# Two sets of product banks in the projections, and two transposing banks and two reciprocal buffers when heads are brought back to nodes

## The reference, cut to what matters

```
# first network (graph convolution)
h = h @ W                                        # here (W1 W2) in one, 256 -> 64, scaled by node
# second and fourth network (attention with H heads of 64; H = 4 and H = 2)
proj = (x @ gat_w.T).reshape(n, H, 64)
s_src = jnp.sum(proj * gat_a_src, -1); s_tgt = jnp.sum(proj * gat_a_tgt, -1)
e     = leaky_relu(s_src[src] + s_tgt[tgt], 0.2);  exp_e = jnp.exp(e - max)
denom = segment_sum(exp_e, tgt)
attn  = exp_e / denom[tgt]
agg   = segment_sum(proj[src] * attn, tgt)       # numerator and denominator are summed apart,
                                                 # and divided once per node
```

## Time and profile before

| | us |
|---|---|
| median of 3 runs (7667.7 to 7686.64) | 7669.45 |
| the profiled execution's own time | 7670.31 |
| its span, first to last instruction | 7668.7 |

### The profile page before, as it was taken

The page is one execution under the profiler, slowest core; times in us unless marked ns, Lnnn a source line. Parts: engine busy times, 40 slices in busy tenths (PEclk is TensorE's granted clock), DMA queues, the critical chain, the costliest instruction groups (busy, mean ns, idle before and its releaser), DMA issues. The chain is left out here.

```text
span 7668.7 us, 88070 instructions
## 1 busy us (share of the span) xinstructions
PE 4482.8 (58%) x19066; PEld 2333.8 (30%) x19067; DVE 4067.2 (53%) x6157; ACT 1802.2 (24%) x2723; POOL 2135.1 (28%) x2216
## 2 busy tenths in 40 slices
PE   4887575309992454549656776556775444430583
PEld 2553574104431122435222333223332121220121
DVE  8976473989984986335222333223331111128895
ACT  1565011108863221334101111001110000010352
POOL 0000000400000000100466665666665666630000
PEclk9998687659995677879777888678886566665797
DMA  1471674326652554235555656555665444453443
GB/s 40 162 235 54 218 252 145 136 85 191 180 159 88 223 220 164 86 103 210 166 163 173 195 186 192 156 161 183 191 203 145 139 136 139 137 134 117 137 134 108
DMA packets 496020, 1197.33 MB, mean 156 GB/s; under 512 B 65578, under 2 KB 288629, under 8 KB 475090
## 3 DMA queue, kind: packets, MB, share of 16 engines
q1 hardware_dynamic: 321342, 586.57, 23.7%
q0 software_dynamic: 141200, 464.73, 20.5%
q10 hardware_dynamic: 33396, 145.09, 5.2%
HBM read 924.69 MB, written 274.66 MB: 156 GB/s over the span
## 5 line engine op out<-in xcount | busy, mean ns | idle before, releaser
L2586 POOL DMA_INDIRECT rel1s_rows<-rel_table,rel1s_at x672 | 651.4, 969 | 396.4 <-issue 349.9
L2586 POOL DMA_INDIRECT rel0s_rows<-rel_table,rel0s_at x672 | 652.1, 970 | 376.1 <-issue 341.1
L2586 POOL DMA_INDIRECT rel2s_rows<-rel_table,rel2s_at x672 | 643.5, 958 | 371.6 <-issue 327.9
L2718 PE MATMUL rel2s_acc<-rel2s_rows,rel2s_hot 128*128 x764 | 407.1, 546 | 471.0 <-issue 409.6
L1677 PE MATMUL gatx_acc<-gatx_w,gatx_feat 128*65 128x400 f32 x1600 | 541.6, 501 | 25.7 <-DVE gatx_w L1569 25.7
L2718 PE MATMUL rel0s_acc<-rel0s_rows,rel0s_hot 128*128 x764 | 349.4, 473 | 295.7 <-issue 231.0
L2718 PE MATMUL rel1s_acc<-rel1s_rows,rel1s_hot 128*128 x764 | 348.5, 472 | 291.9 <-issue 222.1
L2240 POOL DMA_INDIRECT mixa_y<-y_sorted,g_rank x25 | 23.7, 949 | 1532.0 <-issue 1532.0
L2150 PE MATMUL mamb_acc<-mamb_st,g_ident 128*128 128x512 f32 (+1 forms) x448 | 252.5, 729 | 213.9 <-DVE mamb_st L2141 213.9
L1569 DVE SCALAR_TENSOR_TENSOR gatx_w<-gatx_w,gatx_adj 128x1600 f32<-128x1600 f32 x200 | 363.2, 1817 | 0.5 <-ACT gatx_w L1625 0.5
L1416 DVE CUSTOM_DVE_ANT_0 gatm_junk<-gatm_srow,gatm_gone 128x3200 bf16<-128x3200 f32 x100 | 343.5, 3488 | 33.5 <-DMA gatm_srow<-gat_scores 29.1
(11 more groups left out here) (609 smaller groups left out, 9619.5 us busy)
## 6 DMA issues: line engine op xcount, KB each, us to landing
mamb_bc<-dbc SPq DMA_DIRECT2D x64, 1600.0 KB, 6.6
agg_strip<-strips SPq DMA_DIRECT2D x100, 800.0 KB, 5.9
gatx_adj<-adj SPq DMA_DIRECT2D x200, 400.0 KB, 3.1
adj<-adj_counts SPq DMA_DIRECT2D x25, 1600.0 KB, 7.1
latx_adj<-adj SPq DMA_DIRECT2D x100, 400.0 KB, 3.1
rel_table<-rel0p_prod POOLq DMA_DIRECT2D x25, 1536.0 KB, 6.3
rel_table<-rel0s_prod ACTq DMA_DIRECT2D x25, 1536.0 KB
rel_table<-rel1s_prod ACTq DMA_DIRECT2D x25, 1536.0 KB
```

Source lines behind the costliest of these rows:

```text
L2586: pool.indirect_dma_start(rows[:, u, k, :], None, table, bass.IndirectOffsetOnAxis(ap=at[:, n:n + 1], axis=0)).then_inc(s_in[u], 16)
L2718: one = nc.tensor.matmul(acc[a][:, :], to, row[:, 0:2 * D], start=fresh and k == 0, stop=False)
```

## The change

Projections get two sets of product banks, used in turn by the tile's parity. `s_done` starts at `2 * NC`, so that a product waits for DVE's move of tile t-2 in place of t-1; POOL's wait is raised by the same `NC`, so that it still waits for its own tile. In `heads_to_nodes` PE's semaphore `s_o` starts at 1, so that PE waits for tile t-2 in place of t-1, and the reciprocals have a buffer per parity. No instruction is added, removed or put in another order on any engine but the one that sets `s_o`; the lines after 1722 move by up to two.

```
         tp = [ph.ps(f"tp{u}", [P, D]) for u in range(2)]
-        mm = [ph.ps(f"mm{n}", [P, BANK]) for n in range(NC)]
+        mm = [[ph.ps(f"mm{u}_{n}", [P, BANK]) for n in range(NC)] for u in range(2)]
...
             pe.sem_inc(s_tp, 2)
-            pe.sem_inc(s_done, NC)
+            pe.sem_inc(s_done, 2 * NC)
...
                     pe.wait_ge(s_done, t * NC + (n + 1))
                     for k in range(2):
-                        last = nc.tensor.matmul(mm[n][:, 0:b - a], turned[u][:, k, :], weights[:, k, a:b],
+                        last = nc.tensor.matmul(mm[u][n][:, 0:b - a], turned[u][:, k, :], weights[:, k, a:b],
                                                 start=k == 0, stop=k == 1)
...
-                        last = nc.vector.tensor_scalar(res[u][:, a:b], mm[n][:, 0:b - a], scale[:, bass.ds(t, 1)], None, ALU.mult)
+                        last = nc.vector.tensor_scalar(res[u][:, a:b], mm[u][n][:, 0:b - a], scale[:, bass.ds(t, 1)], None, ALU.mult)
...
             def step(t, i, u):
-                pool.wait_ge(s_done, (t + 2) * NC)
+                pool.wait_ge(s_done, (t + 3) * NC)
                 for to, out in store(t, res[u]):
...
         part = [ph.sb(f"part{u}", [65, H, P]) for u in range(2)]
-        den = ph.sb("den", [P, H])
+        dens = [ph.sb(f"den{u}", [P, H]) for u in range(2)]
         tp = [ph.ps(f"tp{u}", [P, BANK]) for u in range(2)]
...
             pe.sem_inc(s_t, 2)
+            pe.sem_inc(s_o, 1)
 
             def step(t, i, u):
                 pe.wait_ge(s_in[u], (i + 1) * 16)
                 pe.wait_ge(s_o, t)
...
             def step(t, i, u):
                 dve.wait_ge(s_t, t + 3)
+                den = dens[u]
```

More of the change, by code:

```diff
@@ L815, in step @@
                         nc.vector.tensor_copy(res[u][:, 0:heads * 65].rearrange("p (h c) -> p h c", c=65)[:, :, 0:64],
-                                              mm[n][:, 0:heads * 64].rearrange("p (h c) -> p h c", c=64))
+                                              mm[u][n][:, 0:heads * 64].rearrange("p (h c) -> p h c", c=64))
                         nc.vector.tensor_copy(extra[:, bass.ds(t, 1), :].rearrange("p a c -> p (a c)"),
-                                              mm[n][:, heads * 64:width])
-                        last = nc.vector.tensor_copy(res[u][:, heads * 65:], mm[n][:, heads * 64:width])
+                                              mm[u][n][:, heads * 64:width])
+                        last = nc.vector.tensor_copy(res[u][:, heads * 65:], mm[u][n][:, heads * 64:width])
                     elif scale is not None:
-                        last = nc.vector.tensor_scalar(res[u][:, a:b], mm[n][:, 0:b - a], scale[:, bass.ds(t, 1)], None, ALU.mult)
+                        last = nc.vector.tensor_scalar(res[u][:, a:b], mm[u][n][:, 0:b - a], scale[:, bass.ds(t, 1)], None, ALU.mult)
                     else:
-                        last = nc.vector.tensor_copy(res[u][:, a:b], mm[n][:, 0:b - a])
+                        last = nc.vector.tensor_copy(res[u][:, a:b], mm[u][n][:, 0:b - a])
                     last.then_inc(s_done, 1)
```

## The result

The changed kernel takes 7658.34 us (median of 20 runs), the kernel before 7670.02 in the same comparison (20 runs). The ratio is 0.9983, 95% interval 0.9976 to 0.9990, so 8 to 18 us less. The profiled execution took 7656.09, its span is 7654.4, 14.3 us under the 7668.7 of before.

A forecast was written before the change was run, and what follows sets the result against it. Bank waits for tile t-1 bounded the stages (`lasp` already its stores), leaving two-buffer load and store loops. Gains 3.6 + 1.4 + 0.5 + 6.2 + 1.3 = 13.0 us gave a median of 7656.5, range 7645 to 7671.

The forecast's parts named there:

- the rival with the Trainium skill's durations: Heads: loads take 2.0 us fixed plus bytes; `lash` gains nothing, `loch` 4.9 us, sum 10.4, median 7659; chance 0.05.
- `locp`: Projection stage: period falls from 1.88 us to its store loop, 3.64 for two tiles or 1.82 each; gain 1.4 us.
- `loch`: Heads stage: period falls from 1.85 us to its load loop, 3.18 for two tiles or 1.59 each; gain 6.2 us.
- the store loop of `gcnp`: Move, POOL's store issue, landing, move two tiles later: 2.95 us for two tiles, 1.48 per tile.
- the load loop of `lash`: Transposes, SP's load issue, landing, transposes two tiles later: 2.62 us for two tiles, 1.31 per tile; gain 1.3 us.
- `gcnp` and `lasp`: Projection stages: `gcnp` from 1.65 to 1.50 us per tile, gain 3.6; `lasp` already at its store loop, 1.77, gain 0.5.
- The banks as the only limit: All five stages: loads and stores follow, DVE bounds the heads and PE the projections; some 67 us, 7602; chance 0.03.
- The full clock in the heads: TensorE leaves 0.50 clock in `loch` and `lash`, transposes about 0.35 us not 0.69; 19 us in all, 7650.5; chance 0.08.
- The lost clock in `locp`: PE stays at 1.2 GHz in `locp`, 2.38 us per tile; 12 us lost in place of 1.4 gained, 7670; chance 0.05.
- The collision: Projections: loads and stores collide on the same 16 DMA engines and land later; 8.0 us slower, 7677.5; chance 0.05.
- my signs of being wrong: `loch`'s transposes name DVE, its loads land under 1.9 us, projections' stores later than 2.6, or untouched stages move over a few us.
- an engine's own work: Floor per tile if banks alone had limited: PE 1.33 us in `gcnp`, DVE 1.0 in `loch` and 0.9 in `lash`.

The follow-up runs named there:

- the second run of the projections alone: Only the projections changed, heads as in the kernel before; second comparison, on another chip: ratio 0.9989 to the kernel before (first comparison 1.0002).
- one buffer of reciprocals: The changed kernel with one reciprocal buffer in the heads, DVE waiting for its own previous multiplication: ratio 0.9979 to the kernel before.
- four result buffers: The changed kernel with four result buffers in the projections, so four stores in flight, and two load buffers: ratio 0.9958 to the kernel before.
- all deep without the change: Four load buffers in all five stages and four result buffers in the projections, but one set of product banks and heads one tile at a time: ratio 0.9986.
- the deep kernel: The changed kernel with four load and four result buffers in the projections and four load buffers in the heads: 7579.52 us against 7669.91, ratio 0.9885.

## Why the prediction was right

**The forecast** was 7656.5 and the measured median 7658.34; the gain forecast 13.0, measured 14.3 in the profiles and 11.7 in the medians. The median alone doesn't bear the mechanism out: its interval, 8 to 18 us, holds the forecast's 13.0 as well as the 10.4 of the rival with the Trainium skill's durations. The waits, the stages and the experiments do. That the sum came so close is in part luck, since two terms missed in opposite directions: `locp` by +1.9 us and `loch` by -0.9.

**The loops.** For two tiles, the store loop of `gcnp` was put at 2.95, that of `locp` at 3.64, the load loop of `lash` at 2.62, and measured are 2.95, 3.65 and 2.61. The one of `gcnp`:

```profile
824.72 0.28 DVE L821 TENSOR_SCALAR gcnp_res<-gcnp_mm,g_dinv 128x64 f32<-128x64 f32 x1 [1.45 <-DMA gcn_y<-gcnp_res]
...
827.67 0.28 DVE L821 TENSOR_SCALAR gcnp_res<-gcnp_mm,g_dinv 128x64 f32<-128x64 f32 x1 [1.41 <-DMA gcn_y<-gcnp_res]
```

For a landing that no view gave I had taken the data's end plus a wait seen elsewhere. In `lash` that held; in `loch` it was 0.13 us too short.

**`loch`** was put at 3.18 and is 3.30: 5.3 us gained in place of 6.2. From the transposes to the issue of the load it takes 0.92 as reckoned; what is longer is from the issue at 2300.61 to the transposes that use it at 2302.99, 2.38 in place of 2.25.

**`locp`** is the term that was mis-sized: 3.3 in place of 1.4 (2.0 to 3.4 over the kernels of the table). The period after was right (1.80 against 1.82); before, I read 1.88 in the middle of the stage where the mean is 1.94. Half of the gain lies in the first period alone. Before, then changed:

```profile
1262.44 0.42 DVE L815 COPY locp_res<-locp_mm 128x256 f32<-128x256 f32 x1 [5.22 <-PE locp_mm L784]
...
1265.29 0.42 DVE L815 COPY locp_res<-locp_mm 128x256 f32<-128x256 f32 x1 [2.28 <-PE locp_mm L784]
```

```profile
1257.92 0.42 DVE L815 COPY locp_res<-locp_mm 128x256 f32<-128x256 f32 x1 [5.22 <-PE locp_mm L784]
1258.02 1.06 PE L784 MATMUL locp_mm<-local_weights,locp_turned 128*128 128x264 f32 x4
...
1259.11 0.42 DVE L815 COPY locp_res<-locp_mm 128x256 f32<-128x256 f32 x1 [0.62 <-PE locp_mm L784]
```

That period falls from 2.85 to 1.19 us, by 1.66; the other 23 give 1.69 together, 0.07 each, where 0.06 was forecast. Of the 1.66, 1.04 is the clock: the second product took 2.10 us at 1.2 GHz before and 1.06 here, where the granted clock was 0.99 from 1257.9 on. It is not shown that the change brings this about. Of the nine kernels with two sets of banks, this product is at full speed in three (the changed one, the second run of the projections alone, one buffer of reciprocals) and takes 1.71 to 1.97 in the others; of the three with one set it takes 1.64 to 2.10. So up to 1 us of the gain may be luck, and the second bank's own part of the first period is some 0.6: 2.20 with a product of 1.97 (four result buffers) against 2.77 with one of 2.02 (all deep without the change). A stage's gain needs its own length, first to last, for the time before, and not the steady period alone.

**`gcnp` and `lasp`**: 3.6 and 0.6 us, put at 3.6 and 0.5. In `gcnp` both periods were read 0.03 us too short (1.65 and 1.50, means of 1.68 and 1.53), which cancels in the difference. `lasp` was said to be at its store loop already; before the change 14 of its 25 moves waited for the store and now 20 do. That its number fits is luck, with a stage that varies by 1.8 us between kernels that are the same there.

**The rivals.** The banks as the only limit: false, but only the deep kernels show by how much, since with four buffers the same banks are worth 77 us (ratios 0.9885 against 0.9986, of 7670), and with two of each 14. The full clock in the heads: `loch` stays at 0.50 even in the deep kernel, with transposes of 0.69. The lost clock in `locp`: it has 0.92 of full in the changed kernel, 0.93 before. The collision: the longest landing of `locp`'s stores did rise, from 2.6 to 3.3, and by its letter that is one of my signs of being wrong, "if the projections' stores land later than 2.6". The sign was badly chosen: before the change `lasp`'s longest was 3.1 already, and what counts over 24 periods is the median, which fell from 2.3 to 2.2. The other signs did not appear: the transposes of `loch` name their load, and the stretches between the touched stages moved by 2.0 us at most. The durations of the Trainium skill: `lash` gained 1.6 us where by them there was nothing to gain. The 2.15 us that I took from "DMA: Bandwidth & Descriptors" of the Trainium skill, "Anatomy of one DMA", is too long for this load by at least 0.1 us. But that section gives its fit for DMAs that GpSimd issues, and SP issues these, so I had no ground for applying it and the miss doesn't speak against the section. For `loch` the same rule came nearer than my own term: 3.29 for two tiles, where I forecast 3.18 and 3.30 was measured.

**My estimate of an engine's own work was too high.** For PE in `gcnp` I had 1.33 and the deep kernel shows 1.16 at the same clock: the overlap of one tile's transposes with the last one's products is larger than I read from the waiting rows. For DVE in `lash` I had 0.9 and it is 0.74. This touched no term of the forecast, but the deep kernel's expectation was 18 us too small in the stages.

## What to carry to other kernels

When a stage is pipelined over tiles, write down every loop that closes over its buffers (bank, load, result), each as its links divided by its number of buffers; a second buffer in one of them is worth the distance to the next longest, and no more. Two loops that lie close hide each other's worth: test the change together with deeper buffers before it is called small. With tiles of about 1 us of work, two buffers were too few for transfers that land some 2 us after their issue: here four in place of two made 0.17% into 1.15%.

## What the runs showed of the hardware

Two buffer loops that run side by side did not settle at equal steps: with two load buffers the tiles came in pairs, 1.11 and 2.19 us apart in `loch`, from the second pair to the end of the stage, and 0.81 and 1.80 in `lash`.

The same kernel took 7670 us on one chip and 7213.4 on another. The touched stages of the projections-alone kernel, which was profiled on a chip of either speed, agree within 1 us; the difference lies in the relational stage, in the idle time between GpSimd's indirect gathers, whose own duration is the same. Here are the kernel before, and the projections-alone kernel on the other chip. The idle time of the gathers that the profile puts down to "issue" is 1018.9 us in the one and 594.4 in the other, 424.5 of the 466 between the two spans (7668.7 and 7202.5):

```profile
L2586 POOL DMA_INDIRECT rel0s_rows<-rel_table,rel0s_at x672: 940/946/1445, 3708.7 to 4722.8; - x168
...
  issue: 1018.9, 1935
```

```profile
L2586 POOL DMA_INDIRECT rel0s_rows<-rel_table,rel0s_at x672: 942/946/1449, 3700.7 to 4551.6; - x168
...
  issue: 594.4, 1951
```

No run tells why, and it stays open. Also on one chip the stretch between `loch` and `lasp`, which nothing here changes, took 4521.7 to 4539.4 us by the profile, more than the whole gain: with such a spread the lengths of the touched stages say more of a change of this size than the total.
